# Cross attention: nine of the 17 key tiles of each pair of heads are transposed on VectorE in 32x32 blocks and put in place by DMA, instead of on TensorE

## What is computed

```python
# context 2048 rows, latents 128 rows, 32 query heads of 128, 4 key/value heads
hidden = concatenate([context, latents], axis=1)          # 2176 rows
q = (latents @ Wq); k = (hidden @ Wk); v = (hidden @ Wv)
scores = einsum("bqhgd,bkhd->bhgqk", q, k) / sqrt(128)
attn = softmax(scores)                                    # 128 x 2176 for each head
out = einsum("bhgqk,bkhd->bqhgd", attn, v) @ Wo
```

## Time and profile before

| | |
|---|---|
| median of three runs | 699.57 us |
| the profiled execution | 698.99 us |
| its span, first to last instruction | 697.3 us |
| TensorE busy | 671.9 us (96%) |
| VectorE / ScalarE / GpSimd busy | 436.9 / 356.7 / 117.1 us |
| mean granted TensorE clock | 0.988 of full speed |
| the 16 attention steps | about 120 to 415 us of the span |

### The profile page before, as it was taken

One profiled execution on the slowest core, in us unless ns is written; L12 is line 12 of the kernel. 1 busy time (PEld: TensorE's weight loads), 2 busy tenths in 40 slices (PEclk: granted clock), 3 DMA queues, 4 the chain that ended last, 5 costly groups with the idle time before them and its releaser, 6 DMA issues.

```text
span 697.3 us, 12695 instructions
## 1 busy us (share of the span) xinstructions
PE 671.9 (96%) x4450; PEld 575.4 (83%) x4450; DVE 436.9 (63%) x1095; ACT 356.7 (51%) x706; POOL 117.1 (17%) x75
## 2 busy tenths in 40 slices
PE   7999998999999999999999987997999999999897
PEld 6888887899999999999999977996797797796453
DVE  2533115767777777677677765779857757756562
ACT  4403116667776677678766652664435435434101
POOL 0000001112431143114321133022220220200100
PEclk9999999999999999999999999998999999999989
DMA  8511001011021110311031503953577667647702
GB/s 257 240 61 60 1 1 61 1 56 67 1 71 52 64 56 0 120 60 60 0 111 50 240 12 145 293 199 144 203 242 264 223 238 274 214 175 276 283 20 98
DMA packets 15701, 87.07 MB, mean 125 GB/s; under 512 B 3584, under 2 KB 3968, under 8 KB 6064
## 3 DMA queue, kind: packets, MB, share of 16 engines
q1 hardware_dynamic: 15088, 85.52, 34.0%
q10 hardware_dynamic: 576, 1.05, 0.5%
HBM read 86.30 MB, written 0.26 MB: 124 GB/s over the span
## 4 chain that ended last, share of the span: by engine, by line
PE 92%; DVE 4%; ACT 2%; DMA 1%; issue 1%; SPq 0%; DVEq 0%; ACTq 0%
PE ps L1284 18%; PE ps L1079 15%; PE ps L1080 15%; PE ps L1081 14%; PE ps L1191 8%; PE ps L1324 8%; PE ps L1148 4%; PE ps L1313 2%; PE ps L1396 2%; PE ps L1431 2%; DMA ring<-wk_dram 1%; PE ps L1295 1%; PE ps L1304 1%; PE ps L1296 1%; DVE acc L922 1%; ACT prob L524 1%
## 5 line engine op out<-in xcount | busy, mean ns | idle before, releaser
L711 DVE TENSOR_TENSOR pt_lo<-ps,pt_hi 128x512 fp32r<-128x512 f32 x144 | 95.1, 661 | 72.0 <-ACT pt_hi L442 71.1
L1284 PEld LDWEIGHTS ps<-norm_t,ring 128*128 128x128 f32 x1152 | 132.6, 193 | 4.8 <-issue 3.9
L1284 PE MATMUL ps<-norm_t,ring 128*128 128x128 f32 x1152 | 133.8, 276 | 0.0
L442 ACT ACTIVATE pt_hi<-ps 128x512 fp32r<-128x512 f32 x144 | 82.2, 571 | 85.0 <-PE ps L1191 84.7
L524 ACT ACTIVATE prob<-prob,neg_max 128x512 f32<-128x512 f32 (+1 forms) x128 | 94.6, 741 | 7.5 <-DVE neg_max L803 7.5
L922 DVE SCALAR_TENSOR_TENSOR acc<-raw,cw,acc 128x127 f32<-128x127 f32 (+2 forms) x240 | 78.5, 402 | 27.9 <-ACT acc L622 27.9
L799 DVE TENSOR_SCALAR_CACHE_REDUCE prob<-ps 128x512 f32<-128x512 f32 (+1 forms) x160 | 92.0, 605 | 2.6 <-PE ps L1081 1.2
L1079 PE MATMUL ps<-pt_hi,v_hi 128*128 128x256 f32 x272 | 88.3, 325 | 0.0
L1191 PE MATMUL ps<-ident,prob 128*128 128x128 f32 x544 | 83.2, 273 | 1.9 <-DVE pt_lo L711 1.3
L1191 PEld LDWEIGHTS ps<-ident,prob 128*128 128x128 f32 x544 | 65.2, 140 | 14.9 <-DVE pt_lo L711 2.2
L1080 PE MATMUL ps<-pt_hi,v_lo 128*128 128x256 f32 x272 | 76.4, 281 | 0.0
(11 more groups left out here) (170 smaller groups left out, 1097.6 us busy)
## 6 DMA issues: line engine op xcount, KB each, us to landing
ring<-w_in_dram SPq DMA_DIRECT2D x36, 1024.0 KB, 4.8
ring<-w_out_dram SPq DMA_DIRECT2D x16, 1024.0 KB, 4.8
ring<-wq_dram SPq DMA_DIRECT2D x8, 1024.0 KB, 5.9
ring<-wo_dram SPq DMA_DIRECT2D x8, 1024.0 KB, 4.8
ring<-w_dram SPq DMA_DIRECT2D x4, 896.0 KB, 6.0
ring<-ctx_t_dram SPq DMA_DIRECT2D x3, 1024.0 KB, 6.8
ring<-w_dram SPq DMA_DIRECT2D x3, 1024.0 KB, 4.7
ring<-wk_dram SPq DMA_DIRECT2D x4, 256.0 KB, 8.2
```

Of the source, the lines that this page charges most:

```text
L442: copy = lambda dst, src: nc.scalar.activation(dst, src, ACT.Copy)
L711: sub = lambda dst, a, hi: nc.vector.tensor_tensor(dst, a, hi, ALU.subtract)
L1284: ins = mm(ps[:, bank, t * T:t * T + T], w[:, t, c, :], norm_t[:, c, :], start=(c == 0), stop=(c == NC - 1))
```

## The change

The key columns are split in two. **Near** are units 0 to 3, key tiles 0 to 7, columns 0 to 1023: they go the old way. **Far** are units 4 to 8, key tiles 8 to 16, columns 1024 to 2175: nine tiles of each head. For pairs 0 to 14 the far columns take this way:

1. ScalarE's exponentials of the far pieces (2 and 3) of a head are moved ahead of those of its near pieces (`EXP_AT`, and the order of the prologue).
2. VectorE transposes the far columns of one head in one instruction of 128x1152 elements, in blocks of 32x32, into `blocks_t` (`turn_far`): head 0 at unit 4, head 1 at unit 6 behind `q_lo`. The first waits until the DMAs of the pair before have landed (`moved`).
3. SyncE waits for both and issues 16 DMAs from SBUF to SBUF (`moves`), each of 32 partitions by 2304 bytes, which carry block row i to block column j into `far_t` (two buffers).
4. ScalarE, at units 2 to 6 of the pair's step, copies far units from `far_t` to `pt_hi`; each copy waits for all 16 DMAs of the pair (`moved`).
5. GpSimd, in place of VectorE, subtracts for `pt_lo` of the far units (`far_split`), and the values of these units wait for it (`pfl_ok`).

TensorE makes no transposes for far units; in the step of pair 15 all units go the old way. `wo_hi` is made at unit 0 instead of 2. GpSimd's `k_lo` and `v_lo` pieces are laid between the far subtractions. The loads of `wq` and `wo` keep their sources and slots and now stand between the groups of 16 DMAs in SyncE's order; the loads of constants and of the state-space weights come after the last group. The transposes of pair n+1 at unit 7 now wait for the seventh of its eight exponentials instead of the fifth.

```diff
-EXP_AT = ((), (), ((0, 0),), ((0, 1), (0, 2)), ((0, 3),), ((1, 0), (1, 1)), ((1, 2),), ((1, 3),), ())
+EXP_AT = ((), (), ((0, 2),), ((0, 3), (0, 0)), ((0, 1),), ((1, 2), (1, 3)), ((1, 0),), ((1, 1),), ())
+
+
+PE_UNITS = 4
+NEAR = 4 * PE_UNITS * P // 2
+FAR = KV_LEN - NEAR
+FAR_T = FAR // P
+FAR_UNITS = UNITS - PE_UNITS
+MOVES = 16
+LAST_PAIR = KVH * PAIRS - 1
...
-W_UNIT = 2
+W_UNIT = 0
...
-                prob = [sbuf(st2, f"prob{b}", [P, 2, KV_LEN]) for b in range(2)]
+                near = [sbuf(st2, f"prob_near{b}", [P, 2, NEAR]) for b in range(2)]
+                far = sbuf(st2, "prob_far", [P, 2, FAR])
+                blocks_t = sbuf(st2, "blocks_t", [P, 4, FAR_T, 2, 32])
+                far_t = [sbuf(st2, f"far_t{b}", [P, 4, FAR_T, 2, 32]) for b in range(2)]
...
+            return near[b][:, h, lo:hi] if lo < NEAR else far[:, h, lo - NEAR:hi - NEAR]
+
+        def far_unit(b, u, w):
+
+            at = 2 * (2 * u - 2 * PE_UNITS)
+            return far_t[b][:].rearrange("p i t h q -> p i (t h) q")[:, :, at:at + 2 * w, :]
+
+        def unit_of(tile, w):
+
+            return tile[:, 0:w, :].rearrange("p w (h i q) -> p i (w h) q", h=2, i=4)
...
+            def moves(m):
+
+                sp.wait_ge(turned, 2 * m + 2)
+                if m >= 2:
+                    sp.wait_ge(pfl_ok, FAR_UNITS * (m - 1))
+                for i in range(4):
+                    for j in range(4):
+                        sp.dma_start(far_t[m % 2][32 * j:32 * j + 32, i, :, :, :],
+                                     blocks_t[32 * i:32 * i + 32, j, :, :, :]).then_inc(moved, 16)
+
+            moves(0)
+            load(2, wq[2], 2)
+            for n in range(LAST_PAIR - 1):
+                kv, p = n // PAIRS, n % PAIRS
+                if p == 2:
+                    load(0, wo[2 * kv + 2], 3 + kv)
+                if p == 0 and kv:
+                    load(1, wo[2 * kv + 1], 2 + kv)
+                moves(n + 1)
+                if p == 1 and kv < KVH - 1:
+                    load(3, wq[2 * kv + 3], 2 + kv)
+                if p == 3 and kv < KVH - 2:
+                    load(2, wq[2 * kv + 4], 3 + kv)
...
+            def far_split(n, u):
+
+                w = 2 if u < 8 else 1
+                pool.wait_ge(pth_ok, UNITS * n + u + 1)
+                sub(unit_of(pt_lo[u % 3], w), far_unit(n % 2, u, w),
+                    unit_of(pt_hi[u % 3], w).bitcast(F32)).then_inc(pfl_ok, 1)
+
+            for n in range(LAST_PAIR + 1):
                 kv, p = n // PAIRS, n % PAIRS
                 more = kv < KVH - 1
                 if more and p == 3:
...
+                for u in range(PE_UNITS, UNITS):
+                    if n < LAST_PAIR:
+                        far_split(n, u)
+                    if more and p == 2 and u == 7:
+                        k_split(kv + 1, 0)
+                    if more and p == 3 and u == 6:
+                        v_split(kv + 1, 0)
                 if more and p == 2:
-                    for i in range(4):
+                    for i in range(1, 4):
                         k_split(kv + 1, i)
                 if more and p == 3:
-                    for part in range(3):
+                    for part in range(1, 3):
                         v_split(kv + 1, part)
...
-                if i == 0:
+                if i == 2:
...
                 w = 2 if u < 8 else 1
-                act.wait_ge(t_ps, unit + 1)
-                copy(pt_hi[u % 3][:, 0:w, :],
-                     ps[:, bank, 0:w * 256].rearrange("p (w n) -> p w n", w=w)).then_inc(pth_ok, 1)
+                if u < PE_UNITS or near_only:
+                    act.wait_ge(t_ps, PE_UNITS * n + u + 1)
+                    copy(pt_hi[u % 3][:, 0:w, :],
+                         ps[:, 4 + u % 2, 0:w * 256].rearrange("p (w n) -> p w n", w=w)).then_inc(pth_ok, 1)
+                else:
+                    act.wait_ge(moved, 16 * MOVES * (n + 1))
+                    copy(unit_of(pt_hi[u % 3], w), far_unit(b, u, w)).then_inc(pth_ok, 1)
...
-            for i in range(NPC):
+            for i in (2, 3, 0, 1):
                 soft_exp(0, 0, 0, i)
-            soft_exp(0, 0, 1, 0)
+            for i in (2, 3, 0):
+                soft_exp(0, 0, 1, i)
             q_split(1, 1, 6)
-            for i in range(1, NPC):
-                soft_exp(0, 0, 1, i)
-            pt_split(0, 0, 4)
-            pt_split(1, 1, 5)
+            soft_exp(0, 0, 1, 1)
...
+            def turn_far(m, h):
+
+                dve.wait_ge(exp_ok, 2 * NPC * m + (2, 6)[h])
+                if h == 0 and not (isinstance(m, int) and m == 0):
+                    dve.wait_ge(moved, 16 * MOVES * m)
+                nc.vector.transpose(blocks_t[:, :, :, h, :].rearrange("p j t q -> p t j q"),
+                                    far[:, h, :].rearrange("p (t j k) -> p t j k", j=4, k=32)).then_inc(turned, 1)
...
+                    if tgt < PE_UNITS or (last and turn and tgt < UNITS):
+                        pt_split(n, tgt)
+                    elif tgt >= UNITS and not (last and turn):
+                        pt_split(n + 1, tgt - UNITS)
...
+                    if u in (4, 6) and not (last and p >= 2):
+                        turn_far(n + 1, (u - 4) // 2)
...
+            turn_far(0, 0)
+            turn_far(0, 1)
             q_split(1, 1, 6)
-            pt_split(0, 0, 4)
-            pt_split(1, 1, 5)
+            pt_split(0, 0)
+            pt_split(0, 1)
...
+            def transposes(m, b, u):
+                if u in (0, 2):
+                    pe.wait_ge(exp_ok, 2 * NPC * m + 7 + u // 2)
...
-            def values(unit, b, u, fresh):
-                pe.wait_ge(ptl_ok, unit + 1)
+            def values(n, b, u, fresh, near_only):
+                if u < PE_UNITS or near_only:
+                    pe.wait_ge(ptl_ok, PE_UNITS * n + u + 1)
+                else:
+                    pe.wait_ge(pfl_ok, FAR_UNITS * n + u - PE_UNITS + 1)
...
+                    if tgt < PE_UNITS or (last and turn and tgt < UNITS):
+                        pe.wait_ge(ptl_ok, PE_UNITS * n + tgt - 1)
+                        transposes(n, b, tgt)
+                    elif tgt >= UNITS and not (last and turn):
+                        pe.wait_ge(ptl_ok, PE_UNITS * n + 2 + tgt - UNITS + 1)
+                        transposes(n + 1, 1 - b, tgt - UNITS)
...
-    nc = bacc.Bacc("TRN2", target_bir_lowering=False, num_devices=1)
+    nc = bacc.Bacc("TRN2", target_bir_lowering=False, num_devices=1, dynamic_dma_scratch_size=1024)
```

More of the change, by code:

```diff
@@ L223, in build @@
         t_ps, pth_ok, ptl_ok, pv_ps = sem("t_ps"), sem("pth_ok"), sem("ptl_ok"), sem("pv_ps")
+        turned, moved, pfl_ok = sem("turned"), sem("moved"), sem("pfl_ok")
         sum_ok, inv_ok, oh_ok, ol_ok = sem("sum_ok"), sem("inv_ok"), sem("oh_ok"), sem("ol_ok")
@@ L385, in _ @@
                 v_split(0, part)
-            for n in range(KVH * PAIRS):
+            def far_split(n, u):
[4 more added lines that the diff above has]
+            for n in range(LAST_PAIR + 1):
                 kv, p = n // PAIRS, n % PAIRS
@@ L550, in attn_step @@
                     tgt = u + 2
-                    if tgt < UNITS or not (last and turn):
+                    if tgt < UNITS:
                         act.wait_ge(pv_ps, 9 * n + u + 1)
-                        pt_split(9 * n + tgt, tgt % UNITS, 4 + (9 * p + tgt) % 2)
+                        pt_split(n, b, tgt, last and turn)
+                    elif not (last and turn):
+                        act.wait_ge(pv_ps, 9 * n + u + 1)
+                        pt_split(n + 1, 1 - b, tgt - UNITS, False)
                     if u == 0 and not first:
@@ L810, in invert, with pt_split @@
                 nc.vector.reciprocal(row_inv[:, b, :], row_sum[:, b, :]).then_inc(inv_ok, 1)
-            def pt_split(unit, u, bank):
+            def pt_split(n, u):
                 w = 2 if u < 8 else 1
-                dve.wait_ge(pth_ok, unit + 1)
-                sub(pt_lo[u % 3][:, 0:w, :], ps[:, bank, 0:w * 256].rearrange("p (w n) -> p w n", w=w),
+                dve.wait_ge(pth_ok, UNITS * n + u + 1)
+                sub(pt_lo[u % 3][:, 0:w, :], ps[:, 4 + u % 2, 0:w * 256].rearrange("p (w n) -> p w n", w=w),
                     pt_hi[u % 3][:, 0:w, :].bitcast(F32)).then_inc(ptl_ok, 1)
+            def turn_far(m, h):
[4 more added lines that the diff above has]
+                                    far[:, h, :].rearrange("p (t j k) -> p t j k", j=4, k=32)).then_inc(turned, 1)
             def o_split(m, b):
@@ L1182, in output @@
                               wo_hi[:, h, :], wo_lo[:, h, :], True, True).then_inc(wo_ps, 1)
-            def transposes(pair, unit, b, u, bank):
-                if u in (2, 4, 6):
-                    pe.wait_ge(exp_ok, 2 * NPC * pair + NPC + u // 2 + 1)
+            def transposes(m, b, u):
+                if u in (0, 2):
+                    pe.wait_ge(exp_ok, 2 * NPC * m + 7 + u // 2)
                 for w in range(2 if u < 8 else 1):
@@ L1190, in transposes @@
```

(20 more changed lines are left out.)

12 lines of the change are left out of this document (6 added, 6 removed).

## The result

The changed kernel takes 752.67 us (median of 4 runs, 749.71 to 754.73) against 699.77 for the kernel before on the same chip: a ratio of 1.0754, interval 1.073 to 1.0778, 53 us slower where 27 were forecast. The profiled execution took 749.71 against 698.99: +50.7. Two single slow runs stay out of all ratios: 2287.72 us in experiment 2, and 976.1 of the kernel before beside experiments 5 to 8.

The account below looks back on a forecast made before the run. TensorE bounded the old kernel; the change was to make a closed loop of waits decide, 9.8 us plus M 10.8, 20.6 a step. Last mark 28.7 later, less 1.6, gave +27.1 and 727 us; range 703 to 775.

Parts of the forecast that it names:

- M: Time from first issue of a pair's 16 DMAs to the last landing: 10.8 us, bounds 9.2 to 14.6.
- the loop: Copy of far unit 4, exponentials, second transpose, 16 DMAs, next pair's copy: a closed wait of 20.6 us a step, chance 0.55.
- what would show it: Signs in the new profile: marks 20.6 us apart, issues 0.5 to 0.6, one TensorE gap of 3 to 4 us a step.
- mark: Start of ScalarE's copy of unit 4 in each step; 18.96 us apart before the change, forecast 20.6.
- one sign of being wrong: Listed against the forecast: a granted clock well under 1 in the attention.
- Mark 0: ScalarE's copy of unit 4 in step 0, behind the prologue: forecast to start at 129.8 instead of 126.35.
- Mark to the transpose's end: The loop without M: ScalarE's copies and exponentials, `q_hi`, `q_lo`, transpose, handovers; 9.8 us, before `v_hi` and `k_hi` pieces.
- The tail: Behind step 14's mark: TensorE's rest of that step shorter by 1.6 us, later parts as before.
- The clock falls: Rival: TensorE at 1.2 GHz behind its gap makes `q_hi` 2.6 us later a loop, +34, 761 us; chance 0.15.
- A fast burst: Rival: the moves issue faster than any pair seen; with M under 7.3 TensorE decides, 670 us; chance 0.15.
- slow transfers: Rival: 32 partitions served slowly, 0.9 us a move, M 15.9, 803 us; chance 0.05.
- slower links: Rival: block transpose at twice its price, +21, or GpSimd at twice its row, +12; 739 to 760 us; chance 0.10.

Follow-up runs that it names:

- experiment 2: Changed kernel with the DMAs of pairs 2 and later carrying three of nine key tiles, output not the reference's: 748.59 us, ratio 1.0675.
- experiments 5 to 8: Changed kernel with 12 filler multiplications 744.31 us; far subtractions on VectorE 769.84; scores, exponentials and transposes reordered 689.35; only exponentials and transposes reordered 742.93.
- experiments 1: Changed kernel with VectorE's low half of the queries put behind the second block transpose: 724.23 us, ratio 1.0337.
- 3: Changed kernel with each pair's bytes in 4 DMAs of 128 partitions instead of 16 of 32, not a usable kernel: 677.84 us, ratio 0.9685.
- experiment 7: Changed kernel with next pair's scores in units 0 to 2, exponentials reordered, both transposes by unit 4, same 16 DMAs: 689.35 us, ratio 0.9851.

## Why the prediction was right, and where its sizes were off

**The mechanism** was as forecast: experiments 1 (a link out: -28), 3 (M down: -75) and 2 (bytes: -4) fit the loop, and none fits bandwidth. The signs named under "what would show it" are there in kind: ScalarE idle before each mark, one gap of TensorE a step (2.5 to 4.5 us), SyncE's queue and DMA in the chain. Two lie outside the figures given, the distance of the marks (22.15 for 20.6) and of the issues (0.63 for 0.5 to 0.6), and one sign of being wrong appeared too: the granted clock was 0.86 in 200 to 250 us.

**The size** was +27.1 forecast and +50.7 in the profiled execution. Its direction and its loop came out of the working; the size is nearly double, and no error made up for another, as all four lie on the same side. The 23.6 between them, by the forecast's own terms:

- *Mark 0*, 129.8 forecast, 132.54 measured: +2.7. 0.7 because the first exponential already starts 0.7 later than in the kernel before (113.74 for 113.03) and so does the fifth (116.68 for 115.98 in the earlier trace rows), for a cause that I have not traced; 2.0 because the first 16 issues took 11.25 us, 0.70 each, and M was 12.8.
- *M*, 10.8 forecast. The undisturbed one is 11.52: fifteen intervals of 0.63 where I took 0.56, 9.4, and a landing of 2.1 where I took 2.4. The mean over the loops is 11.71, as the last two have 12.35 and 12.69, which I have not traced. 0.91 in 14 loops: +12.8. The interval of 0.63 stood in the earlier trace rows, at the rows with few partitions, which these moves resemble; I had gone to the middle. This is the step that was mis-sized most.
- *Mark to the transpose's end*, 9.96 forecast as a mean with `v_hi` and `k_hi`, 10.44 measured: +6.8 in 14 loops. These are waits that the sum did not have, behind TensorE at the lower clock: 6.1 us for `neg_max`, and 0.8 of `q_hi` for the queries, in steps 1 and 4. The links themselves were nearly exact: 9.8 by the sum, 9.66 in steps 8 and 12, which have neither these waits nor `k_hi` or `v_hi`.
- *The tail*, -1.6 forecast, -0.3 measured (the last mark +51.0, the whole +50.7): +1.3.

**The rivals.** *The clock falls* was half right and I had it as all or nothing: it happens at 12 of 15 gaps, and it costs 0.5 a step in the mean and not 2.6. I had put it on the queries ahead of `q_hi`, and there it strikes in two steps, 0.34 and 0.50:
```profile
228.85 0.39 ACT L501 ACTIVATE q_hi<-ps 128x256 fp32r<-128x256 f32 x1 [0.50 <-PE ps L1228]
```
Most of it is at the scores ahead of `neg_max`, 1.0 us where it strikes fully. The Trainium skill, TensorE: Matmul & The Clock Gate, "HAM oscillation — how this bites in real kernels", has every burst behind such a DMA wait start at the lower clock. This kernel bears it out in part: at 12 gaps, such as the one at 242, the clock was down when TensorE started or within 1.2 us of that, and at three, such as that of 3.2 us at 264, it stayed up. *A fast burst* is excluded by the interval, *slow transfers* and *slower links* by the view of the tile. The estimate of 2.8 us from the Trainium skill's 311 ns (VectorE: DVE Perf Modes, "The three transpose paths") stands against 1.38 measured for nine float32 tiles. The move was not hidden behind TensorE's work in this order, and is in that of experiment 7.

## What to carry to other kernels

Before work goes to an engine or a queue of its own, write down who waits for it in order, what stands behind the waiting instruction, and whether that leads back to the work: then the length of that loop, not the sum of any engine, is the price, and it can be shortened by reordering calls alone (28 us by moving two lines, 63 by starting the loop's work ahead of the wait). Find all paths that close it before cutting one. Count the issues of a move in many small DMAs on one queue: here they cost some 0.6 us each, far more than their bytes.

## What the hardware showed that I had not expected

- Issues on SyncE's queue are 0.63 us apart at 24 KB and 72 KB over 32 partitions, and 0.61 at 288 KB over 128. Landing within SBUF took 1.8, 2.1 and 2.6 us for 24, 72 and 288 KB.
- A block transpose of 128x1152 float32 on VectorE took 1.38 us, close to the 1.4 worked out from subtractions.
- TensorE's clock fell at 12 of 15 gaps of 2.5 to 4.5 us in the same loop, and the length of the gap does not tell which.
- A float32 multiplication of 128x128 by 128x128 is two records of 0.115 us at full clock, so a filler of 12 calls lasts 2.8 us.
